# Layer-norm rows turned by SBUF transfers and VectorE 32x32 blocks instead of TensorE, in a pre-norm attention + FFN kernel

## The reference

```
x = x + softmax((ln(x)Wq'+bq)(ln(x)Wk'+bk)' / 16 * gaussian_mask) (ln(x)Wv'+bv) Wo' + bo
x = x + gelu(ln(x) bw1' + b1) bw2' + b2        # bw = mean|w| * sign(w), hidden size 1024
```

## Time and profile before

| | |
|---|---|
| median of three runs | 1504.25 us |
| profiled execution, its own time | 1503.99 us |
| span of the profile | 1502.2 us |
| TensorE busy | 1475.3 us (98%) |
| VectorE busy | 1030.4 us (69%) |
| GpSimd busy | 834.7 us (56%) |
| ScalarE busy | 785.1 us (52%) |

### The profile page before, as it was taken

The page is one execution under the profiler, slowest core; times in us unless marked ns, Lnnn a source line. Parts: engine busy times, 40 slices in busy tenths (PEclk is TensorE's granted clock), DMA queues, the critical chain, the costliest instruction groups (busy, mean ns, idle before and its releaser), DMA issues.

```text
span 1502.2 us, 24033 instructions
## 1 busy us (share of the span) xinstructions
PE 1475.3 (98%) x9421; PEld 1330.7 (89%) x9421; DVE 1030.4 (69%) x1681; ACT 785.1 (52%) x951; POOL 834.7 (56%) x1097
## 2 busy tenths in 40 slices
PE   8999999999999999999999999999999999999997
PEld 6788989999898998989899898998989989899986
DVE  7567776767767677675776767667675677767574
ACT  5554654645556454564646546465564646546342
POOL 3564637556364673637646375573646746375553
PEclk9999999999999999999999999999999999999999
DMA  5422413224131332403314132342313324131330
GB/s 189 78 36 43 127 24 75 72 57 113 32 75 63 71 99 43 114 24 75 85 46 124 29 70 71 61 109 43 91 36 78 92 43 127 22 75 45 57 85 28
DMA packets 86060, 106.16 MB, mean 71 GB/s; under 512 B 9390, under 2 KB 77372, under 8 KB 85948
## 3 DMA queue, kind: packets, MB, share of 16 engines
q1 hardware_dynamic: 85920, 104.63, 29.3%
q10 hardware_dynamic: 28, 0.01, 0.0%
HBM read 20.72 MB, written 16.78 MB: 25 GB/s over the span
## 4 chain that ended last, share of the span: by engine, by line
PE 89%; DMA 3%; DVE 2%; SPq 2%; ACT 2%; issue 2%; POOL 1%; POOLq 0%
PE ps L886 22%; PE ps L1072 15%; PE ps L925 8%; PE ps L924 8%; PE ps L904 7%; PE ps L906 7%; PE ps L905 7%; DMA prob<-prob 2%; PE ps L872 2%; PE ps L871 2%; PE ps L870 2%; PE ps L932 2%; PE ps L853 2%; PE ps L854 2%; PE ps L856 2%; PE ps L837 2%
## 5 line engine op out<-in xcount | busy, mean ns | idle before, releaser
L319 POOL TENSOR_TENSOR ptl<-pt,pth 128x512 fp32r<-128x512 f32 x256 | 326.7, 1297 | 198.1 <-ACT pth L457 198.1
L904 PE MATMUL ps<-vh,pth 128*128 128x258 f32 x1024 | 294.2, 287 | 3.2 <-POOL ptl L319 3.2
L337 POOL TENSOR_TENSOR xin<-xin,ys 128x256 f32<-128x256 f32 x128 | 94.6, 740 | 359.0 <-DVE ys L665 358.9
L906 PE MATMUL ps<-vh,ptl 128*128 128x258 f32 x1024 | 290.7, 284 | 0.0
L905 PE MATMUL ps<-vl,pth 128*128 128x256 f32 x1024 | 289.3, 283 | 0.0
L457 ACT ACTIVATE pth<-pt 128x1024 fp32r<-128x1024 f32 x128 | 135.8, 1061 | 268.3 <-DVE pt L612 268.3
L924 PE MATMUL ps<-sgn,gh 128*128 128x256 f32 x1024 | 248.6, 281 | 5.9 <-DVE gl L647 5.9
L925 PE MATMUL ps<-sgn,gl 128*128 128x256 f32 x1024 | 248.2, 285 | 0.0
L606 DVE TENSOR_REDUCE nmax<-ps 128x1 f32<-128x1024 f32 x128 | 156.4, 1222 | 118.9 <-PE ps L886 118.9
L444 ACT ACTIVATE prob<-ps,nmax 128x1024 f32<-128x1024 f32 x128 | 142.6, 1114 | 179.7 <-DVE nmax L606 179.4
L612 DVE STREAM_TRANSPOSE pt<-prob 128x1024 f32<-128x1024 f32 x128 | 158.8, 1240 | 84.6 <-DMA prob<-prob 84.5
(11 more groups left out here) (116 smaller groups left out, 2799.8 us busy)
## 6 DMA issues: line engine op xcount, KB each, us to landing
prob<-prob SPq DMA_DIRECT2D x512, 128.0 KB, 3.4
xin<-in_L_attn_x_dram SPq DMA_DIRECT2D x32, 512.0 KB, 4.8
out_dram<-xin SPq DMA_DIRECT2D x31, 512.0 KB, 4.0
w1s<-in_L_ffn_w_dram SPq DMA_DIRECT2D x1, 1024.0 KB, 10.4
w2s<-in_L_ffn_w_dram SPq DMA_DIRECT2D x1, 1024.0 KB, 12.5
mask_bc<-mask_dram SPq DMA_DIRECT2D x1, 512.0 KB, 7.4
out_dram<-xin SPq DMA_DIRECT2D x1, 384.0 KB, 2.4
wk<-in_L_attn_Wk_dram SPq DMA_DIRECT2D x1, 256.0 KB, 5.1
```

Source lines behind the costliest of these rows:

```text
L319: pool.tensor_tensor(ptl[:, q % P_SLOTS, half(n)], pt[:, q % P_SLOTS, half(n)], pth[:, q % P_SLOTS, half(n)].bitcast(F32), ALU.subtract).t ...
L904: pe.matmul(with_sum, pth[:, q % P_SLOTS, tile(j)], vh[:, j, :], start=j == 0, stop=False)
L906: last = pe.matmul(with_sum, ptl[:, q % P_SLOTS, tile(j)], vh[:, j, :], start=False, stop=j == T - 1)
```

## The change

The normalised rows of the second and later batches, and the second norm's rows of all but the last batch, no longer pass through TensorE. ScalarE writes them in an order keyed by 32 columns, SyncE regroups them with four transfers for each half (16 more for each batch), and VectorE turns the blocks (`turn_x`, `turn_x2`) into SBUF tiles `xt` and `x2t`. The high parts, low parts and masked keys then read these SBUF tiles, not PSUM. The first batch's first norm and the last batch's second norm keep the old way. The transfers of the first norm land in `kmf`, those of the second in the first buffer of the exponentials.

The first FFN layer runs by pairs of hidden blocks over one half of the tokens, first half first, behind all the values. Of the eight pairs GpSimd takes the low part of pairs 0 and 3 (`lo_hidden`), between its bias additions, and VectorE that of the other six. The masked keys are made by two instructions, not one. The rest of the diff moves calls in the five programs.

```diff
+POOL_PAIRS = (0, 3)
 # SyncE
+            def regroup_x(b, n):
+                sp.wait_ge(xn1_set, T * b + TH * (n + 1))
...
+                for i in range(P // QUAD):
+                    sp.dma_start(kmf[i * QUAD:(i + 1) * QUAD, n, :],
+                                 xn1_keyed[:, n, i]).then_inc(x_back[n], 16)
+            def regroup_x2(b, n):
+                sp.wait_ge(xn2_set, T * b + TH * (n + 1))
...
+                for i in range(P // QUAD):
+                    sp.dma_start(exps(0)[i * QUAD:(i + 1) * QUAD, :],
+                                 xn2_keyed[:, n, i]).then_inc(x2_back[n], 16)
             def batch(b, more):
-                for q in range(TH, T):
+                if more:
+                    regroup_x(b + 1, 0)
+                regroup_probs(b, 4)
+                if more:
+                    regroup_x(b + 1, 1)
+                for q in range(5, T):
                     regroup_probs(b, q)
+                if more:
+                    for n in range(N2):
+                        regroup_x2(b, n)
...
 # GpSimd
+            def lo_hidden(b, k):
+                n, js = pair_of(k)
+                ts = slice(n * TH, (n + 1) * TH)
+                pool.wait_ge(gh_set, J * b + k + 1)
+                for m, j in enumerate(range(js.start, js.stop)):
+                    val = g[:, k % G_SLOTS, half(m)].rearrange("p (t c) -> p t c", t=TH)
+                    last = pool.tensor_tensor(gl[:, ts, j, :], val, gh[:, ts, j, :].bitcast(F32), ALU.subtract)
+                last.then_inc(glp_set, 1)
                 rstd_ffn(b, 6)
+                rstd_ffn(b, 7)
                 if more:
                     split_keys(b + 1, range(1, 2))
-                rstd_ffn(b, 7)
-                add_b2(b, s)
+                add_b2(b, s, range(TH))
+                if more:
+                    lo_hidden(b, 0)
+                add_b2(b, s, range(TH, T))
+                if more:
+                    lo_hidden(b, 3)
 # VectorE
+            def turn_x(b, n):
+                dve.wait_ge(x_back[n], 64 * b)
+                dve.transpose(xt[:, n].rearrange("p t c (l g h) -> p g (t c) h l", g=P // QUAD, h=P // QUAD),
+                              kmf[:, n, :].rearrange("p (g k r) -> p g k r", g=P // QUAD, r=QUAD)).then_inc(xt_set, 1)
             def lo_rows(b, n):
                 dve.wait_ge(xh_set, N2 * b + n + 1)
-                dve.tensor_tensor(xl[:, :, half(n)], slot(n), xh[:, :, half(n)].bitcast(F32),
+                dve.tensor_tensor(xl[:, n], from_banks(slot(n)) if b == 0 else xt[:, n], xh[:, n].bitcast(F32),
                                   ALU.subtract).then_inc(xl_set, 1)
...
                     if q < TH - 1:
                         turn_probs(b, q + 3)
+                    if more and q in (1, 2):
+                        turn_x(b + 1, q - 1)
...
                 turn_probs(b, 6)
+                mask_keys(b + 1, 0)
                 lo_rows(b + 1, 0)
                 add_attention(b, s, 4)
-                mask_keys(b + 1, 0)
                 lo_rows(b + 1, 1)
                 turn_probs(b, 7)
...
                 add_attention(b, s, 6)
+                turn_x2(b, 0)
                 lo_queries(b + 1, range(2, QG))
                 add_attention(b, s, 7)
-                lo_rows_ffn(b, 0, x2l[:, 0], slot(0))
-                lo_values(b + 1, range(0, 3))
-                lo_rows_ffn(b, 1, x2l[:, 1], slot(1))
-                lo_values(b + 1, range(3, VG))
+                lo_rows_ffn(b, 0)
+                lo_values(b + 1, range(VG))
                 dve.wait_ge(kl_set, N2 * (b + 2))
-                for j in range(J):
-                    split_column(b, j)
+                turn_x2(b, 1)
+                split_pair(b, 0)
+                lo_rows_ffn(b, 1)
+                for k in range(1, J):
+                    split_pair(b, k)
                 head(b + 1, b)
 # ScalarE
                     normalize_ffn(b, s, 1)
+                    hi_rows(b + 1, 0)
...
                 normalize_ffn(b, s, 2)
-                hi_rows(b + 1, 0)
+                hi_rows(b + 1, 1)
...
+                gelu_pairs(b, range(0, 1))
+                hi_rows_ffn(b, 1)
+                gelu_pairs(b, range(1, J))
 # TensorE
-                turn_rows(b + 1, 0)
                 weigh_values(b, 4)
-                turn_rows(b + 1, 1)
                 weigh_values(b, 5)
                 queries(b + 1, range(0, 2))
                 weigh_values(b, 6)
                 queries(b + 1, range(2, QG))
                 weigh_values(b, 7)
...
-                turn_rows_ffn(b, 0, 0)
-                values(b + 1, range(0, 3))
...
-                turn_rows_ffn(b, 1, 2)
-                values(b + 1, range(3, VG))
...
+                values(b + 1, range(VG))
+                hidden_pairs(b, range(J))
```

More of the change, by code:

```diff
@@ L176, in preln_attention_ffn @@
         p_back = [sem(f"p_back{k}") for k in range(QUEUED)]
+        xt_set, x2t_set, glp_set = (sem(n) for n in ("xt_set", "x2t_set", "glp_set"))
+        x_back = [sem(f"x_back{n}") for n in range(N2)]
+        x2_back = [sem(f"x2_back{n}") for n in range(N2)]
         stats2, aggr2, vareps2, rstd2_set, xn2_set, b2_added = (
@@ L197, in tile, with from_banks, pool_splits, splits_up_to @@
             return slice(t * P, (t + 1) * P)
+        def from_banks(ap):
+            return ap.rearrange("p c (t q) -> p t c q", q=P)
+        def pool_splits(b, k):
+            return b < B - 1 and k in POOL_PAIRS
+        def splits_up_to(b, k):
+            dve = sum(not pool_splits(d, i) for d in range(b + 1) for i in range(J if d < b else k + 1))
+            return dve, J * b + k + 1 - dve
         def exps(q):
@@ L708, in last_tail @@
                 normalize_ffn(b, s, 3)
-                lo_rows_ffn(b, 0, kl[:, :, half(0)], slot(0))
+                lo_rows_ffn(b, 0)
                 turn_probs(b, 7)
@@ L723, in last_tail @@
                 scale_outputs(b, range(1, 2))
-                lo_rows_ffn(b, 1, kl[:, :, half(1)], slot(0))
+                lo_rows_ffn(b, 1)
                 scale_outputs(b, range(2, 4))
@@ L931, in turn_rows_ffn @@
                     for c in range(C):
-                        last = pe.transpose(ps[:, bank + c, tile(t)], xn2[:, TH * n + t, tile(c)], ident[:])
+                        last = pe.transpose(ps[:, c, tile(t)], xn2[:, TH * n + t, tile(c)], ident[:])
                 last.then_inc(x2_turned, 1)
@@ L945, in hidden_pairs @@
                         for c in range(C):
-                            for part in (x2h, kl):
-                                last = pe.matmul(ps[:, 2 + 2 * (k % 2) + m, :], sgn1[:, c, tile(j)], part[:, c, half(n)],
-                                                 start=c == 0 and part is x2h, stop=c == C - 1 and part is kl)
+                            for part in (x2h, x2l):
+                                last = pe.matmul(ps[:, 2 + 2 * (k % 2) + m, :].rearrange("p (t q) -> p t q", q=P),
+                                                 sgn1[:, c, tile(j)], part[:, n, :, c, :],
+                                                 start=c == 0 and part is x2h, stop=c == C - 1 and part is x2l)
                     last.then_inc(hidden, 1)
@@ L1054, in batch @@
                 weigh_values(b, 7)
-                pe.wait_ge(km_set, N2 * (b + 1) + 1)
-                turn_rows_ffn(b, 0, 0)
-                values(b + 1, range(0, 3))
-                pe.wait_ge(km_set, N2 * (b + 2))
-                turn_rows_ffn(b, 1, 2)
-                values(b + 1, range(3, VG))
-                for j in range(J):
-                    if j == 0:
-                        pe.wait_ge(vl_set, VG * (b + 1) + 2)
-                    if j >= 2:
-                        pe.wait_ge(gelu_set, J * b + j - 1)
-                    order = [(c, lo, n) for c in range(C) for lo in (False, True) for n in range(N2)]
-                    if j == 0:
-                        order.sort(key=lambda cpn: cpn[2])
-                    for k, (c, lo, n) in enumerate(order):
-                        if j == 0 and k % 4 == 0:
-                            pe.wait_ge(x2l_set, N2 * b + n + 1)
-                        last = pe.matmul(ps[:, 4 - 2 * (j % 2) + n, :], sgn1[:, c, tile(j)],
-                                         x2l[:, n, c, :] if lo else x2h[:, c, half(n)],
-                                         start=c == 0 and not lo, stop=c == C - 1 and lo)
-                    last.then_inc(hidden, 1)
+                values(b + 1, range(VG))
+                hidden_pairs(b, range(J))
                 scores(b + 1, 0)
```

155 lines of the change are left out of this document (93 added, 62 removed).

## The result

The changed kernel takes 1614.23 us, the median of four runs (1610.18 to 1619.04), beside 1504.26 us for the kernel before: a ratio of 1.073, 95% interval 1.0699 to 1.076. It is slower, as forecast, but by 110 us and not 55, and 32 us beyond the range.

What follows compares the result with a forecast made beforehand. TensorE's stream (busy 98%) was taken as the bound. Steps A to C made a batch 3.7 us longer, not 3.5 shorter: 1504 + 15 x 3.7 = 1559 us; own range 1525 to 1582, wider range 1492 to 1582.

Steps and rivals of the forecast that it cites:

- The two rivals on the faster side: Whole kernel: collisions rare or short, 1498 us, chance 0.16; or all of TensorE's saving arrives, 1452 us, chance 0.09.
- Step A: From a batch's last scores (s7) to the end of the last weighing group (w7): w7 ends 1.2 us late.
- The probabilities' transfers behind the rows' transfers: In Step A, tile 5's four transfers queue behind four of `regroup_x`: 0.7 us lost by issuing.
- The scattered turns: In Step A, `turn_x` of the second half: taken at 1.24 us, possibly 1.2 to twice that.
- rival 3: Scattered turns take twice 1.24 us: 1.2 more in Step A and in Step B, 1595 us; chance 0.05.
- Exclusion at masks and low rows: In Step A, VectorE and GpSimd shut each other out at masks and low rows: 0.4 to 0.8 us a batch.
- Step B: From w7 to the second norm's turned second half: hidden pairs start at 742.5 (742.96 before), turned half ready at 747.6.
- Step C: Splitting of hidden pairs: VectorE's 13.8 and GpSimd's 7.8 us add, FFN row 0 at 768.8 instead of 765.1.

Runs made afterwards that it cites:

- r3: The changed kernel with the first norm's eight transfers a batch carrying 4 KB each instead of 128 KB, its turn reading the mask row: 1579.5 us.
- r2: The changed kernel with the four added turns of a batch writing rows of 32 elements without gaps, not scattered: 1582.18 us.
- r7: The kernel before, with low rows and masked keys of the second and later batches computed from the mask row in SBUF, not from PSUM: 1512.35 us.
- r9: The changed kernel with the edits of r2, r3 and r5 together: 1525.88 us.
- r4: The kernel before, with the changed kernel's GpSimd work added in the splitting of the hidden blocks, its results unused: 1561.15 us.
- r1: The changed kernel with GpSimd splitting no hidden pair, VectorE taking the low parts of all eight: 1599.29 us.
- r5: r1 with ScalarE taking GELU pair 1 ahead of the high part of the second token half: 1562.62 us.
- r8: The kernel before, with only the second norm's first half by transfers and a turn, and the last root ahead of the low keys: 1495.47 us.

## Why the prediction was half right

**The sign** held, and with it the reason that TensorE's stream was full: its saving could only arrive if other chains became shorter, and they became longer. The two rivals on the faster side fail: the subtraction (L739) has a mean of 1.53 us, not 1.23, and TensorE's busy share fell to 92%. In the two batches above the waits are 7.6 and 8.3 us (98.62 − 90.99, 96.75 − 88.44), where 5 to 8 were forecast. They stand at the queries and the hidden pairs, as named, but none at FFN row 0, where the forecast had the splitting hold TensorE last.

**The step that failed is Step A**, "w7 ends at 736.7, 1.2 late". By the table it was 0.79 (transposes) + 15.66 (w4 to w7) + 2.88 (w7) = 19.33 us before and 20.74 + 2.94 = 23.68 after: 4.35 us more. The 3.15 above the forecast are 47 us over 15 batches, nearly the whole error of 55. By its terms:

- *The probabilities' transfers behind the rows' transfers.* Priced at 0.7 us for one tile, by the issuing alone. Measured 2.2 us from exponential to turn, for two tiles one behind the other, 1 of it the issuing and 1.2 the bytes. In r3, with the bytes gone, Step A is 2.2 us shorter, of which 0.8 is clock. This is the largest term. It shows first at q0, for the low rows of the first half, a wait that the forecast names among its signs but gives no size.
- *The scattered turns.* Bounded as 1.2 us to twice that and taken at 1.24; measured 1.98 and 2.03. r2: Step A is 1.2 us shorter, and the time 32 us. This was rival 3, with a chance of 0.05 and 36 us above the forecast. I set it beside the forecast as another case, though both could come true together, and did.
- *Exclusion at masks and low rows.* Half a microsecond a batch by r7, no more than was reckoned.
- *The clock.* No term at all. 1.4 us of clock loss lie in this step, where it was 0.1 before. After the waits at q0 and q2 the stages q0-w6 and q2-w7, which hold no new work and no wait, are 0.37 and 0.79 longer.

With short turns and without the bytes (r9) Step A is still 1.8 us longer than before, 0.8 of it clock; the 1.0 left is beside the 1.2 of the forecast.

**Step B** was right in when the hidden pairs begin: from w7's end 7.48 us before, 5.8 forecast (736.7 to 742.5), 5.75 measured. The turned second half is ready 6.2 us behind the first hidden matmul where 5.1 was forecast (747.6 − 742.5); 0.8 of that is the scattered turn. (The forecast's own terms add up to 740.6 for the last row, not 740.4, which changes nothing.) Pair 3 waits 2.8 us for it in most batches, in place of "some 2".

**Step C** came out right by luck. Forecast +4.2 us from the start of the hidden pairs to the first FFN row, measured +4.46. The price of the exclusion was sound: VectorE's splitting ends 26.0 us behind the first hidden matmul, 26.3 by the forecast, and r4 shows that the exclusion costs 3.7 us, clock included, where nothing else is wrong. But that is not what holds TensorE here: the 4.46 are 2.9 us of waiting, nearly all for the GELU behind the late half, and 1.5 of clock loss; TensorE thereby reaches the 13th matmul of FFN row 0 at 25.2 + 1.4 = 26.6, behind the end of the splitting. So two causes of nearly the same length lie side by side. r1 takes out one and brings 15 us; r5 takes out both and brings 52. The prediction named the second and hid it under the first without pricing it by itself. The remaining combination, GELU pair 1 first with GpSimd's pairs kept, was not run, so how long the exclusion alone would hold the changed kernel is not shown; r4 shows it for the kernel before.

The steps as measured, 4.35 − 1.73 + 4.46 = 7.1 us a batch, make up the 7.2 of the period. The clock is spread over them: 46 us by the account at the top, 0.029 x 1612.6 = 47 by the mean granted clock (0.995 to 0.966), 45 by the clock loss, 3 us a batch. It has no place in the prediction's sum.

## What to carry to other kernels

A full engine is relieved by another path only where that path has slack: move the one piece whose input is ready early and whose consumer is late (r8, −9 us), not the whole operation (+110 us). A transfer put ahead of a critical one costs its time on the way as well as its time of issue; and when a sum says that one cause hides another, price the hidden one alone, since removing the first may bring nothing. Where a change makes TensorE wait, look at the granted clock behind each wait: it is a cost of its own, and here independent work that filled the wait made the kernel faster.

## What the runs showed of the hardware that I had not expected

- A VectorE turn of 32x32 blocks, 128x1024 in float32, takes 2.03 us with writes scattered at a step of four elements, 1.98 at a step of sixteen, and 1.24 with rows of 32 in one piece (r2: 1.23).
- The granted clock can fall to half behind waits of TensorE of 2 to 3 us in an otherwise full stream, and need not: at one place of r1 it fell in eight of twelve batches with waits of 2.76 to 2.82 us, for 3.4 us each, and was 0.50 for some 6 us behind one of 3.05; in one batch of the changed kernel it fell 1.4 us behind a wait of 1.88 us that followed one of 2.55. Busy time doesn't show it: the slow windows read 2.00 of 2.00.
- VectorE's cast beside GpSimd goes from 0.69 to 1.78 us, and subtractions from 1.23 to 2.19, for one GpSimd instruction of 128x512 waited out.
- Matmuls whose moving operand is four runs of 128 columns start every 0.235 us at full clock (r1, 794 to 796), as those with 512 in one piece did before (15.27 us for 64, 0.239 each).
